# A ring of eight slots and early Gelu in a graph attention, and products of zeros around two routing stages

## The reference

```python
# layer 0 attention, on the layer-normed x
Wh = X @ W.T
e = s_i[:, None] + s_j[None, :];  e = where(e >= 0, e, 0.2 * e)
attention = softmax(where(A == 0, -inf, e), axis=1)
x = x + gelu(attention @ Wh)
# then in both layers, on the layer-normed x
logits = x @ gate_w + gate_b          # 8 experts
top2 of softmax(logits) -> two experts and two weights per node
x = x + sum of weight * expert(x)     # gelu(x @ W1 + b1) @ W2 + b2
```

## Time and profile before

| what | value |
|---|---|
| median of 3 runs | 1987.38 us (1985.22 to 1990.87) |
| the profiled execution | 1985.19 us, span 1983.5 us |
| TensorE, weight loads, VectorE, ScalarE, GpSimd busy | 84%, 77%, 50%, 52%, 17% of the span |
| mean granted clock of TensorE | 0.92 |
| first attention | 143.4 to 455.4 us |
| from its last product to the first turn of routing, layer 0 | 29.4 us, TensorE idle |
| routing loop, layer 0 and layer 1 | 31.3 us each, clock 0.50 |

### The profile page before, as it was taken

One profiled execution on the slowest core, in us unless ns is written; L12 is line 12 of the kernel. 1 busy time (PEld: TensorE's weight loads), 2 busy tenths in 40 slices (PEclk: granted clock), 3 DMA queues, 4 the chain that ended last, 5 costly groups with the idle time before them and its releaser, 6 DMA issues. The chain is left out here.

```text
span 1983.5 us, 42662 instructions
## 1 busy us (share of the span) xinstructions
PE 1663.3 (84%) x12926; PEld 1536.0 (77%) x12927; DVE 1000.5 (50%) x2248; ACT 1030.1 (52%) x2127; POOL 329.1 (17%) x282
## 2 busy tenths in 40 slices
PE   4639999994679999294997988979965899999998
PEld 3538888883569999174997988979965799999997
DVE  4638888786622222477776776766767011111011
ACT  1634444443335555015877887878842445455453
POOL 1100000000037766000000000000000333333332
PEclk9959999996589999597998999989966899999999
DMA  9960000003357777500000000000044666666664
GB/s 149 108 129 14 8 16 8 21 0 111 111 151 203 202 205 189 167 0 19 11 8 17 16 15 12 13 12 17 8 154 154 211 179 182 183 185 183 176 179 106
DMA packets 81362, 190.01 MB, mean 96 GB/s; under 512 B 9562, under 2 KB 52854, under 8 KB 72470
## 3 DMA queue, kind: packets, MB, share of 16 engines
q1 hardware_dynamic: 48438, 138.73, 21.2%
q0 software_dynamic: 27280, 45.56, 14.3%
q10 hardware_dynamic: 5584, 4.99, 0.8%
HBM read 189.37 MB, written 33.11 MB: 112 GB/s over the span
## 5 line engine op out<-in xcount | busy, mean ns | idle before, releaser
L1256 PE MATMUL bank<-arena 128*128 128x195 bf16 x5408 | 479.1, 250 | 74.5 <-DVE arena L1116 46.6
L1256 PEld LDWEIGHTS bank<-arena 128*128 128x128 fp8e4 x5408 | 469.8, 98 | 83.8 <-issue 81.8
L1021 ACT ACTIVATE arena<-arena,m_row 128x512 fp8e5<-128x512 f32 (+1 forms) x728 | 429.4, 677 | 101.8 <-DVE arena L1116 89.7
L1708 PEld LDWEIGHTS bank<-X,arena 128*128 128x128 f32 x2832 | 338.5, 194 | 5.9
L1708 PE MATMUL bank<-X,arena 128*128 128x128 f32 x2832 | 338.9, 277 | 0.0
L1805 DVE TENSOR_TENSOR arena<-bank,X 128x256 f32<-128x256 f32 x118 | 50.1, 424 | 557.1 <-PE bank L1746 557.1
L1746 PE MATMUL bank<-arena,X 128*128 x1416 | 327.6, 381 | 1.7 <-ACT X L1781 1.7
L884 PE MATMUL bank<-arena 128*128 (+1 forms) x1352 | 300.3, 384 | 15.9 <-DVE arena L827 15.9
L884 PEld LDWEIGHTS bank<-arena 128*128 128x128 f32 x1352 | 257.5, 191 | 57.8 <-issue 21.8
L1746 PEld LDWEIGHTS bank<-arena,X 128*128 128x128 f32 x1416 | 259.8, 190 | 39.0 <-issue 8.4
L805 ACT ACTIVATE bank<-arena,s_all 128x384 f32<-128x384 f32 (+1 forms) x234 | 133.9, 573 | 185.0 <-DVE arena L819 176.5
(11 more groups left out here) (205 smaller groups left out, 1325.8 us busy)
## 6 DMA issues: line engine op xcount, KB each, us to landing
arena<-m1w SPq DMA_DIRECT2D x67, 1024.0 KB, 4.9
arena<-m0w SPq DMA_DIRECT2D x67, 512.0 KB, 4.0
arena<-adjT POOLq DMA_DIRECT2D x26, 416.0 KB, 13.0
xs<-X SPq DMA_DIRECT2D x4, 1664.0 KB, 6.9
arena<-qd SPq DMA_DIRECT2D x25, 256.0 KB, 3.2
xe<-zeros POOLq DMA_DIRECT2D x1, 3456.0 KB, 14.7
X<-x_in SPq DMA_DIRECT2D x2, 1664.0 KB, 11.1
xd<-X SPq DMA_DIRECT2D x13, 256.0 KB, 2.1
```

What stands on the lines that cost most here:

```text
L1021: last = a.activation(self.sign[slot].bitcast(F8W)[:, q * W:q * W + nt * P], self.row[r][:, 0:nt * P], ACT.Sigmoid, scale=STEEP, bias=self ...
L1256: last = pe.matmul(bank[r * NT + n][:, kind * KW:(kind + 1) * KW], self.split[slot][kind].bitcast(F8)[:, q * W + n * P:q * W + (n + 1) * P ...
L1708: last = pe.matmul(bank[2 * s + c // 4][:, c % 4 * P:(c % 4 + 1) * P], self.W1[s][:, k * HID + c * P:k * HID + (c + 1) * P], self.rxt[s][: ...
```

## The change

It does five things.

1. The first attention has eight probability slots instead of four (`RING = 8`), and its loops run over eight chunks a turn instead of four. The order of `larger` and `masked` stays, and the division of the block before still stands after chunk 3.
2. The Gelu of the output pairs is no longer all at the end: ScalarE does pairs 0 to 3 after block 3, pairs 4 to 8 after block 6, and pairs 9 to 12 after block 8. After each of the first two batches it runs one exponential over a spare word (`exp_again`).
3. VectorE adds the pairs to X (`add_pairs`) and makes their statistics (`stats_of`) inside the attention, behind the first eight chunks of a block: adds of pairs 0 to 3 in block 5, their statistics in block 6, adds of pairs 4 to 6 in block 7, their statistics in block 8; the rest after block 8. Routing of layer 0 then leaves out its own statistics; routing of layer 1 keeps them (`done=not self.second_norm`).
4. At the end of the first attention TensorE runs 32 products of zeros (128x512, bf16) into a bank that nobody reads.
5. In routing TensorE runs such products after the gate is loaded (4 in layer 0, 32 in layer 1) and one behind each chunk's gate product (26 in each layer).

```diff
+IDLE_PRODUCTS = 32
...
-                self.slots = 2 if H > 1 else 4
+                self.slots = 2 if H > 1 else self.RING
...
+            RING = 8
...
+            def gelu_pairs(self, a, first, last):
+
+                for i in range(first, last):
+                    o = self.attn_out[:, i * 2 * D:(i + 1) * 2 * D]
+                    a.activation(o, o, ACT.Gelu).then_inc(self.out_ready, 1)
...
+                def exp_again():
+                    a.activation(self.exp_spare, ones_t[:, 0:1], ACT.Exp)
+
+                for b in range(4):
+                    block_of(b, self.nt)
+                a.wait_ge(self.banks_free[0], 3)
+                self.gelu_pairs(a, 0, 4)
+                exp_again()
+                for b in range(4, 7):
+                    block_of(b, self.nt)
+                a.wait_ge(self.banks_free[1], 4)
+                self.gelu_pairs(a, 4, 9)
+                exp_again()
+                block_of(7, self.nt)
+                block_of(8, self.L.tail // P)
+                a.wait_ge(self.banks_free[1], 5)
+                self.gelu_pairs(a, 9, 12)
+                a.wait_ge(self.banks_free[0], 6)
+                self.gelu_pairs(a, 12, PAIRS)
...
+                def add_pairs(first, last):
+                    for i in range(first, last):
+                        v.wait_ge(self.out_ready, i + 1)
+                        xs_ = X[:, i * 2 * D:(i + 1) * 2 * D]
+                        v.tensor_tensor(xs_, xs_, self.attn_out[:, i * 2 * D:(i + 1) * 2 * D], ALU.add
+                                        ).then_inc(self.x_added, 1)
+
+                def stats_of(first, last):
+                    for i in range(first, last):
+                        v.wait_ge(self.x_added, i + 1)
+                        for t in (2 * i, 2 * i + 1):
+                            v.bn_stats(stats[:, t * 6:t * 6 + 6], X[:, t * D:(t + 1) * D]).then_inc(stat, 1)
...
+                    larger(b, nt, 0, 0, 0)
+                    for q in range(R):
+                        larger(b, nt, q + 1, (q + 1) % R, (q + 1) // R)
                         masked(b, nt, q, q, 0)
...
+                        if q == 3 and b > 0:
+                            normalise(b - 1, nt_)
+                    if b == 5:
+                        add_pairs(0, 4)
+                    if b == 6:
+                        stats_of(0, 4)
+                    if b == 7:
+                        add_pairs(4, 7)
+                    if b == 8:
+                        stats_of(4, 7)
...
+                add_pairs(7, 9)
+                stats_of(7, 9)
+                add_pairs(9, 12)
+                stats_of(9, 12)
+                normalise(L.blocks, L.tail // P)
+                add_pairs(12, PAIRS)
+                stats_of(12, PAIRS)
...
+                pe.wait_ge(self.banks_free[1], L.blocks // 2 + 1)
+                with pe.Fori(0, IDLE_PRODUCTS):
+                    pe.matmul(bank[5][:, :], zeros[:, 0:P], zeros[:, :], start=True, stop=True)
...
-                layer_norm_stats(v, self)
+                layer_norm_stats(v, self, done=not self.second_norm)
...
                     last.then_inc(self.lg_done, 1)
-
+                    idle_product()
+
+                def idle_product():
+                    pe.matmul(bank[6][:, :], zeros[:, 0:P], zeros[:, :], start=True, stop=True)
+
+                with pe.Fori(0, IDLE_PRODUCTS if self.second_norm else 4):
+                    idle_product()
                 turn(0, 0)
```

More of the change, by code:

```diff
@@ L274, in __init__ @@
                     k += T * D
+                    self.exp_spare = words(k, 1)
+                    k += 1
                 assert k <= ARENA, (tag, k)
@@ L840, in normalise @@
                     last.then_inc(self.banks_free[r], 1)
-                def body(b, bp, r, nt, earlier_block=None):
-                    larger(b, r, nt, 0, 0, 0)
-                    for q in range(4):
-                        larger(b, r, nt, q + 1, (q + 1) % 4, (q + 1) // 4)
-                        masked(b, nt, q, q, 0)
-                    if earlier_block is not None:
-                        normalise(*earlier_block)
-                    with v.Fori(1, T // 4) as i:
-                        for q in range(4):
-                            larger(b, r, nt, 4 * i + q + 1, (q + 1) % 4, i + (q + 1) // 4)
-                            masked(b, nt, 4 * i + q, q, i)
-                    n = T // 4
-                    larger(b, r, nt, T - 1, 1, n)
-                    for q in range(2):
-                        masked(b, nt, 4 * n + q, q, n)
-                    v.wait_ge(self.prob_ready[1], (b + 1) * 7)
-                    v.sem_inc(self.rows_free[r], 1)
@@ new lines, in stats_of, with block_of @@
+                def stats_of(first, last):
[3 more added lines that the diff above has]
+                            v.bn_stats(stats[:, t * 6:t * 6 + 6], X[:, t * D:(t + 1) * D]).then_inc(stat, 1)
+                def block_of(b, nt):
+                    larger(b, nt, 0, 0, 0)
+                    for q in range(R):
+                        larger(b, nt, q + 1, (q + 1) % R, (q + 1) // R)
+                        masked(b, nt, q, q, 0)
+                        if q == 3 and b > 0:
[8 more added lines that the diff above has]
+                        stats_of(4, 7)
+                    n = T // R
+                    with v.Fori(1, n) as i:
+                        for q in range(R):
+                            larger(b, nt, R * i + q + 1, (q + 1) % R, i + (q + 1) // R)
+                            masked(b, nt, R * i + q, q, i)
+                    larger(b, nt, T - 1, 1, n)
+                    for q in range(2):
+                        masked(b, nt, R * n + q, q, n)
+                    v.wait_ge(self.prob_ready[1], (b + 1) * self.ring_uses(1))
+                    v.sem_inc(self.rows_free[b % 2], 1)
@@ L871, in single_tensor @@
+                for b in range(L.blocks):
+                    block_of(b, nt_)
+                block_of(L.blocks, L.tail // P)
+                add_pairs(7, 9)
[5 more added lines that the diff above has]
+                stats_of(12, PAIRS)
             def single_tensor(self, pe):
@@ L891, in single_tensor @@
                 self.each_block(pe, body)
-            def gelu_scalar(self, a):
-                a.wait_ge(self.banks_free[0], self.L.blocks // 2 + 1 + 1)
-                for i in range(PAIRS):
-                    o = self.attn_out[:, i * 2 * D:(i + 1) * 2 * D]
-                    a.activation(o, o, ACT.Gelu).then_inc(self.out_ready, 1)
-            def gelu_vector(self, v):
-                with v.Fori(0, PAIRS) as i:
-                    v.wait_ge(self.out_ready, i + 1)
-                    xs = X[:, at(i * 2 * D, 2 * D)]
-                    v.tensor_tensor(xs, xs, self.attn_out[:, at(i * 2 * D, 2 * D)], ALU.add
-                                    ).then_inc(self.x_added, 1)
+                pe.wait_ge(self.banks_free[1], L.blocks // 2 + 1)
+                with pe.Fori(0, IDLE_PRODUCTS):
+                    pe.matmul(bank[5][:, :], zeros[:, 0:P], zeros[:, :], start=True, stop=True)
             def gelu_sync(self, sp):
@@ L1935, in _ @@
             def _(v):
-                A0.single_vector(v)
-                A0.gelu_vector(v)
+                A0.single_vector(v, X0.stat)
             @block.scalar
```

49 lines of the change are left out of this document (22 added, 27 removed).

## The result

The changed kernel takes 1976.66 us (median of 8 runs, 1963.78 to 1980.56), the kernel before 1988.24 (8 runs, 1985.22 to 1990.87). The ratio is 0.9935, 95% interval 0.9915 to 0.9954. The profiled execution took 1978.46 us against 1985.19, so 6.7 less. The medians differ by more, 11.6 us: the profiled execution before is the fastest of its eight runs, that of the changed kernel lies 1.8 above its median. The forecast was 1973, its range 1956 to 1988.

A forecast was written before the change was run, and what follows sets the result against it. TensorE was taken as the bound, losing time to idle stretches and half clock in the routing loops. Terms 4.4 - 9.1 - 6.9 + 7.3 - 7.9 = -12.2 took 1985.2 to 1973 us, range 1956 to 1988.

The forecast's parts named there:

- Eight slots: First attention: the 0.92 us wait at each block's start stays, slots alone give 0; they buy cover, 7 us of lead.
- Adds and statistics: First attention, blocks 5 to 8: partly covered by VectorE's lead, costing 1.1, 1.4, 0.5 and 1.4, sum +4.4 us (0 to 8.9).
- Gelu batches: ScalarE's batches between attention blocks: hidden by the 7 us lead, 0; about 2 us each if the lead were only 3.
- sign 1: In blocks 5 to 7 TensorE waits once more, 0.5 to 1.4 us, behind VectorE's adds and statistics; 2 to 3 if uncovered.
- The tail: End of the first attention's stage: 8.5 us after the last product instead of 17.6, -9.1 us, with the 32 products hidden.
- sign (3): Attention's stage ends 8 to 9 us after its last product, with a store as last event, not a product of zeros.
- Start of layer 0: Routing of layer 0: first turn after 4.9 us instead of 11.8, -6.9 us; the products of zeros cost 1.7 here.
- Loop of layer 0: Routing loop, layer 0: clock stays at half, each product of zeros adds 0.28 us, 26 of them +7.3 us.
- Rival A: Full clock in layer 0's routing loop too, if the idle stretch is too short to lose it: 1957 us, chance 0.12.
- Start of layer 1: Routing of layer 1: the 32 products of zeros end as VectorE's statistics do, nothing on the path (3.7 if clock never rose).
- Loop of layer 1: Routing loop, layer 1: starts and stays at full clock, 0.87 us a tile instead of 1.17, -7.9 us.
- Rival B: Turns don't hold the clock, lost some tiles into layer 1's loop: +5.8 instead of -7.9, 1986.6 us, chance 0.14.

The follow-up runs named there:

- the last experiment: Changed kernel with zero products written out, ten before the gate, others around picks and first turns, eleven in layer 0's Gelu pause: 1954.66 us, 0.9834 of the kernel before.

## Why the prediction was right, and where it was off

The sign, the range and the likeliest case held, and the two loops came at the clocks that were forecast: 39.8 us at 0.50 in layer 0 (forecast 38.6) and 23.6 at 1.00 in layer 1 (forecast 23.4). The median is 3.7 us above the forecast, the profiled execution 5.5. That the medians differ by 11.6 us, almost the 12.2 of the sum, is in part luck: term by term the traces give 6.7. Step by step:

*Eight slots.* "The slots alone give 0" was not tested by itself. In the kernel before TensorE waits once more four chunks into a block, as here in block 6, and in blocks 1 to 6 alike:

```profile
360.53 5.46 PE L884 MATMUL bank<-arena 128*128 x24 [0.92 <-DVE arena L827]
366.17 28.86 PE L884 MATMUL bank<-arena 128*128 x132 [0.17 <-DVE arena L827]
```

These six waits, 1.0 us in all, are gone, and the prediction had no term for them. It isn't the slots that took them away, for the run with four slots has none either. They stand where VectorE ran two blocks a turn of a loop; block 7, written out in the kernel before, has none, and now all blocks are written out. The other reading of the step, that the ring buys the cover, is open, as said above.

*Adds and statistics.* Forecast costs 1.1, 1.4, 0.5, 1.4, sum 4.4. Measured in the changed kernel, against the same blocks of the run that has them behind block 8: 1.2, 1.4, 0.6, 1.4, sum 4.6. The cover was reckoned right (the wait itself is shorter than the cost, in block 7 0.32 us, below the 0.5 of sign 1). The attention ends only 1.6 later all the same: 1.0 is the six waits, 0.9 an earlier start (142.5 instead of 143.4), and 1.2 a shorter block 0, in which the clock rose sooner (0.78 instead of 0.51 in the mean of 143.4 to 149.5). The last two are in no step and not owed to the change: with the old attention and only products of zeros added the start is 143.0 and block 0 0.9 us shorter than before. Gelu batches: 0, as forecast; the 2 us a batch reckoned for four slots was too much, since that run shows 0.2 for both.

*The tail.* -8.5 for -9.1, but for another reason than the one given: sign (3) was wrong. The step "32 x 0.21 = 6.8 us" priced the product and not the loop around it. With 13 of them at 0.385 us a piece they end last, where the store would have ended the stage 7.7 us after the last product, as it does in the runs without these products or with them written out.

*Start of layer 0.* 5.7 instead of 4.9 (the step's own terms, 3.5 and 1.7, make 5.2): the gate's bias lands 4.1 us after the stage's start, not 3.5: it is issued 0.45 us into the stage and lands 3.6 later, where the earlier trace rows has 3.0 as the median of both layers. The four products took 1.64, as reckoned.

*Loop of layer 0.* The mechanism was right, the size 0.05 us a product too small: (39.78 - 31.26) / 26 = 0.33 where 0.28 was taken. Rival A's condition was as narrow as said: the clock was still at 1.00 when the gate landed and fell 0.2 us later. That the forecast's case came and not A's is in part luck, and two of the eight runs look like A. Ten products in the pause give the other case, 1962 where A had said 1957.

*Start of layer 1.* Forecast 0, measured +2.5. The same mis-sized term as in the tail: 32 products take 12.5 us, not 9.8, and here they stand on the path. Written out they take 9.5.

*Loop of layer 1.* -7.7 for -7.9. Rival B fell, and its mechanism with it: two turns and the gate products of a tile alone lose the clock, two turns more hold it.

*What is in no step.* +2.2 us in the first expert tiles of layer 0 and +0.8 behind the loop of layer 1: after the loop the stretches of full and half clock lie otherwise against the work than before. The prediction treated all that follows a loop as shifted. The part in the first tiles of layer 0 scatters by some 4 us between the kernels here, and the trace of the last experiment has the pause and the tiles behind it at full clock.

## What to carry to other kernels

Work that keeps TensorE's clock up pays only where it stands in the pause ahead of the slow stretch and reaches up to it; the same products inside a stretch at half clock are pure cost, 0.33 us each here. Once the clock is up, something in the stretch must hold it: here one product of zeros, or two turns, a tile. Price such products with the loop around them: in a loop of one they came 0.385 us apart, written out 0.21 at full clock. Work moved into an engine with time to spare is cheap only as far as that engine is ahead: with four slots and right behind the division the 8.9 us of adds and statistics cost their whole length, with eight slots and four chunks later 4.5 us. And when one edit brings a deeper ring, blocks written out and another place for the work, take them apart before you credit one of them.

## What the runs showed of the hardware

Turns in 32 bits hold the clock: 24.2 us at 1.00 with four turns a tile, where with two it fell after 5.5 us. How soon the clock comes back differs from case to case: with the ten and four products behind an idle 7.7 us it was at 0.50 for 3 of the 6.0 us up to the first turn (mean 0.75), with the 32 of layer 1, whose first came 3.1 us into the stage, for 6.9 of 15.7 (mean 0.78). From the last product with W1 in layer 0 to the routing of layer 1, which no kernel here touches, the profiled executions took 660.6 to 665.4 us, a scatter as large as several of the effects studied.
